# Three-pass products in the output projections and the last graph layer, a mask turned earlier, one transfer asked for earlier

## The reference

```python
x = x + L0_gnn(layernorm(x))    # relu(batchnorm(mean of neighbours @ W_l.T + x @ W_r.T)) + x
x = x + L0_ffn(layernorm(x))    # causal attention, 8 heads of 64:  y = o @ Wo, then a soft mixture of 8 experts
x = x + L1_gnn(layernorm(x))    # 2 graph attention layers:  attn = agg @ Wo[l].T + bo[l]; batchnorm(x + attn) ...
x = x + L1_ffn(layernorm(x))    # 8 experts, top 2 of 8
x = x + L2_gnn(...); x = x + L2_ffn(...)
x = x + L3_gnn(layernorm(x))    # xw = x @ W.T;  out = A_norm @ xw;  gelu(batchnorm(out)) + x
x = x + L3_ffn(layernorm(x))    # 8 experts, top 2 of 8, hidden size 1536
```

## Time and profile before

| | us |
|---|---|
| median of 3 runs (1652.82, 1652.84, 3165.91) | 1652.84 |
| the profiled execution | 1647.62 |
| its span | 1645.4 |
| PE busy | 1580.1 |
| DVE busy | 1233.9 |
| ACT busy | 942.8 |
| POOL busy | 293.5 |

### The profile page before, as it was taken

The page is one execution under the profiler, slowest core; times in us unless marked ns, Lnnn a source line. Parts: engine busy times, 40 slices in busy tenths (PEclk is TensorE's granted clock), DMA queues, the critical chain, the costliest instruction groups (busy, mean ns, idle before and its releaser), DMA issues.

```text
span 1645.4 us, 26288 instructions
## 1 busy us (share of the span) xinstructions
PE 1580.1 (96%) x8703; PEld 1246.9 (76%) x8703; DVE 1233.9 (75%) x2122; ACT 942.8 (57%) x1584; POOL 293.5 (18%) x276
## 2 busy tenths in 40 slices
PE   9997998999999999989999999999999999999998
PEld 8885765878876887568788765865778888888886
DVE  8836662455756475799999868453899999999997
ACT  1423373433644363359999563421578878778784
POOL 0023731010210021198000302000550000000003
PEclk9998998999999999999999999999999999999999
DMA  8010000022001000254952330005264348935003
GB/s 339 20 35 17 1 2 13 1 117 77 1 2 39 1 2 13 116 185 159 343 186 89 102 141 0 1 1 230 63 234 160 130 160 357 390 134 209 19 19 100
DMA packets 42240, 173.15 MB, mean 105 GB/s; under 512 B 10219, under 2 KB 10472, under 8 KB 26681
## 3 DMA queue, kind: packets, MB, share of 16 engines
q1 hardware_dynamic: 28742, 153.75, 24.5%
q0 software_dynamic: 8960, 10.29, 2.3%
q10 hardware_dynamic: 4464, 8.13, 1.3%
HBM read 275.54 MB, written 19.25 MB: 179 GB/s over the span
## 4 chain that ended last, share of the span: by engine, by line
PE 80%; DVE 12%; issue 3%; ACT 2%; DMA 1%; POOL 1%; DVEq 0%; SPq 0%; ACTq 0%; POOLq 0%
PE bank L1097 10%; PE bank L1093 10%; PE bank L1094 10%; PE bank L947 4%; PE bank L919 4%; PE bank L994 4%; PE bank L907 3%; PE bank L859 3%; PE bank L1043 3%; PE bank L1331 3%; PE bank L1223 3%; PE bank L878 2%; PE bank L1396 2%; PE bank L1119 2%; PE bank L1305 2%
## 5 line engine op out<-in xcount | busy, mean ns | idle before, releaser
L719 POOL DMA_INDIRECT sb_W<-slots_out,sb_slus x20 | 30.1, 1503 | 544.8 <-DMA slots_out<-sb_rC 539.3
L1557 ACT ACTIVATE sb_rF<-sb_rF,sb_nmx 125x625 f32<-125x625 f32 (+4 forms) x120 | 89.5, 746 | 45.0 <-DVE sb_nmx L2112 44.9
L657 POOL TENSOR_TENSOR sb_rstd<-sb_ve,sb_half 125x3 f32<-125x3 f32 (+4 forms) x29 | 24.9, 859 | 447.9 <-DVE sb_ve L2016 241.6
L385 DVE TENSOR_TENSOR sb_rA_r<-sb_W,sb_rA_r 128x1024 fp32r<-128x1024 f32 x68 | 83.3, 1226 | 12.1 <-ACT sb_rA_r L1670 12.0
L794 PE MATMUL bank<-sb_ones 128*128 128x512 f32 x184 | 88.5, 628 | 3.8 <-DVE sb_rC L2702 1.3
L2112 DVE CUSTOM_DVE_ANT_0 sb_rF<-bank,sb_rG 125x625 f32<-125x625 f32 x80 | 61.5, 806 | 36.0 <-PE bank L907 35.2
L385 DVE TENSOR_TENSOR sb_rB_r<-sb_W,sb_rB_r 128x1024 fp32r<-128x1024 f32 x68 | 83.4, 1227 | 0.1
L385 DVE TENSOR_TENSOR sb_XT_r<-sb_W,sb_XT_r 128x1024 fp32r<-128x1024 f32 x68 | 83.0, 1220 | 0.2 <-ACT sb_XT_r L1670 0.2
L1670 ACT ACTIVATE sb_rA_r<-sb_W 128x1024 fp32r<-128x1024 f32 x68 | 71.5, 1052 | 14.5 <-DMA sb_W<-in_w_m 11.8
L1705 ACT ACTIVATE sb_rG_r<-bank 128x512 fp32r<-128x512 f32 x51 | 30.5, 598 | 82.0 <-PE bank L1119 82.0
L947 PE MATMUL bank<-sb_rA,sb_rDE 125*64 125x125 f32 x1040 | 69.2, 276 | 4.6 <-DVE sb_rA L2126 4.3
(11 more groups left out here) (549 smaller groups left out, 4795.0 us busy)
## 6 DMA issues: line engine op xcount, KB each, us to landing
sb_W<-in_w_m SPq DMA_DIRECT2D x204, 1024.0 KB
sb_rDE<-in_w_m SPq DMA_DIRECT2D x17, 1024.0 KB
sb_rC<-slots_in SPq DMA_DIRECT2D x33, 256.0 KB, 2.7
sb_W<-in_w_g SPq DMA_DIRECT2D x8, 1024.0 KB, 4.9
slots_out<-sb_rC ACTq DMA_DIRECT2D x31, 256.0 KB, 2.0
slots_in<-sb_rC SPq DMA_DIRECT2D x1, 4608.0 KB, 24.8
sb_W<-in_w_a SPq DMA_DIRECT2D x4, 1024.0 KB, 17.5
sb_W<-in_w_m SPq DMA_DIRECT2D x2, 2048.0 KB, 16.9
```

The costliest lines, as they stand in the source:

```text
L385: eng.tensor_tensor(lo, src[:, HALF * h:HALF * (h + 1)], hi.bitcast(F32), ALU.subtract).then_inc(split(r, p, h, b, "lo")[0], 1)
L1557: act.activation(SM[:, s % 4, 0:kn], SM[:, s % 4, 0:kn], ACT.Exp, scale=-1.0, bias=nmx[:, s:s + 1], accum_out=dens[:, s:s + 1]).then_inc(S ...
```

## The change

- `project_output` replaces `project([(Wo, OT)], ...)` in three places. It multiplies in three passes. OT is split in place at the end of `attention` (`output_high` on ACT, `output_low` on DVE): two pieces of 2 chunks for the tokens that are done, ahead of the last pair's steps, and one for the last tile after the last normalising. Wo is split chunk by chunk in the pair loop, on ACT at p = 5, 7, 9, 11 and on DVE at p = 6, 8, 10, 12. PE starts with a group that does not need the last tile (in the causal case group 1), and asks for the last piece ahead of its second group.
- The last graph layer: ACT and DVE split XT, W3 and AT (W3's high part after the mixture), PE makes both products in three passes; the first product's output is split as it is evicted.
- The mask: 13 of the 25 tiles are turned between groups 2 and 3 of the feature products, with ACT's logarithms after its third eviction, and groups 4 to 7 wait for the bank that each needs; 12 are turned after the last eviction, in place of three `keep` products. The second turning, its wait for `rows_vec` and five further `keep` products go, and eight come after the wait for the logarithms.
- `weights(("y", 0), 1, ...)` is asked for ahead of the scatter wait and `nodes(2)`.

```diff
@@ blocks
                 weights(("a", 1), 1, e, new)
+                weights(("y", 0), 1, e, new)
                 sp.wait_ge(S("sc"), 16 * 2 * T * (r // 2 + 1))
                 nodes(2)
-                weights(("y", 0), 1, e, new)
@@ tensor
+            def project_output(causal, a, full):
+
+                first = 1 if causal else 0
+                pe.wait_ge(S("ot_lo"), a * OT_STEPS + C + 2)
+                for i, j in enumerate((first, 1 - first) + tuple(range(2, len(GROUPS)))):
+                    m, lo, hi = GROUPS[j]
+                    if i == 1:
+                        pe.wait_ge(S("ot_lo"), a * OT_STEPS + C + 3)
+                    n = hi - lo + (hi - lo) % 2
+                    for c in range(C):
+                        for w, x in ((Wo_hi[causal], OT_hi[causal]), (Wo_hi[causal], OT_lo), (Wo_lo, OT_hi[causal])):
+                            mm = pe.matmul(bank[:, j, 0:n], w[c][:, m * P:(m + 1) * P], x[:, c, lo:lo + n],
...
+            def mask_tiles(a, b):
+
+                for at, first, end in MASK_PARTS[a:b]:
+                    for f in range(first, end):
+                        t, k = divmod(f, T)
+                        mm = pe.transpose(bank[0:R, at, (f - first) * P:(f - first) * P + R], AT[:, k, t * R:(t + 1) * R], ident[0:R, 0:R])
+                    mm.then_inc(S("msk_pe"), 1)
+
             for j, (m, lo, hi) in enumerate(GROUPS):
+                if j == 3:
+                    mask_tiles(0, 4)
+                if j >= 4:
+                    pe.wait_ge(S("msk_act"), j - 3)
...
             pe.wait_ge(S("h_done"), 8)
-            keep(7, 3)
+            mask_tiles(4, 7)
+            keep(4, 1)
             to_rows(HB, S("rows_full"), S("bn_out"), 0)
-            keep(7, 2)
-
-            pe.wait_ge(S("rows_vec"), 2 * T)
-            for t in range(T):
-                for k in range(T):
-                    mm = pe.transpose(bank[0:R, t, k * P:k * P + R] if k < 4 else bank[0:R, 5 + t // 4, t % 4 * P:t % 4 * P + R],
-                                      AT[:, k, t * R:(t + 1) * R], ident[0:R, 0:R])
-                mm.then_inc(S("msk_pe"), 1)
-
-
-            keep(7, 3)
-            pe.wait_ge(S("msk_act"), 2 * T)
+            pe.wait_ge(S("msk_act"), len(MASK_PARTS))
+            keep(7, 8)
+
             ln_to_feats(1)
...
+            pe.wait_ge(S("mw_hi"), L3W + 1)
+            for c in range(C):
+                pe.wait_ge(S("mx_hi"), L3X + c + 1)
+                for t in range(T):
+                    pe.matmul(bank[0:R, t, :], x3[0][:, c, t * R:(t + 1) * R], w3[0][:, c], start=(c == 0), stop=False)
+                pe.wait_ge(S("mx_lo"), L3L + c + 1)
+                for t in range(T):
+                    pe.matmul(bank[0:R, t, :], x3[1][:, c, t * R:(t + 1) * R], w3[0][:, c], start=False, stop=False)
+            pe.wait_ge(S("mw_lo"), L3W + 1)
             for t in range(T):
-                row_group(t, XT, t, W3, S("xw_full"))
-            pe.wait_ge(S("xw_done"), 2 + T)
+                for c in range(C):
+                    mm = pe.matmul(bank[0:R, t, :], x3[0][:, c, t * R:(t + 1) * R], w3[1][:, c], start=False, stop=(c == C - 1))
+                mm.then_inc(S("xw_full"), 1)
+            pe.wait_ge(S("mx_hi"), L3X + C + T)
+            pe.wait_ge(S("mx_lo"), L3L + C + T)
             for j, (m, lo, hi) in enumerate(GROUPS):
+                n = hi - lo + (hi - lo) % 2
                 for k in range(T):
-                    mm = pe.matmul(bank[:, j, 0:hi - lo], XW[:, k, m * P:(m + 1) * P], AT[:, k, lo:hi], start=(k == 0), stop=(k == T - 1))
+                    if j == 0:
+                        pe.wait_ge(S("xw_done"), 2 + k + 1)
+                        pe.wait_ge(S("mx_lo"), L3L + C + T + k + 1)
+                    for a, b in ((0, 0), (1, 0), (0, 1)):
+                        mm = pe.matmul(bank[:, j, 0:n], xw3[a][:, k, m * P:(m + 1) * P], at3[b][:, k, lo:lo + n],
@@ scalar, exps
+                    if p == PAIRS:
+                        act.wait_ge(S("at_s"), base(ATT) + ATT)
+                        output_high(0)
+                        output_high(1)
                     if 1 <= p <= PAIRS:
                         turned(p - 1)
                     if p >= 3 and p % 2 == 1:
                         weights((p - 3) // 2)
                     if 1 <= p < PAIRS:
                         exp(2 * p + 1)
+                    if p in (5, 7, 9, 11):
+                        c = (p - 5) // 2
+                        act.wait_ge(S("ld_p3"), base(16) + 16)
+                        act.activation(Wo_hi[causal][c], Wo[:, c], ACT.Copy).then_inc(S("ot_hi"), 1)
+                output_high(2)
@@ vector, attention
                     if 1 <= p <= PAIRS:
                         turned(p - 1)
+                    if p == PAIRS:
+                        output_low(0)
+                        output_low(1)
                     if p >= 3 and p % 2 == 1:
                         normed((p - 3) // 2)
+                    if p in (6, 8, 10, 12):
+                        c = (p - 6) // 2
+                        dve.wait_ge(S("ot_hi"), done + c + 1)
+                        dve.tensor_tensor(Wo_lo[c], Wo[:, c], Wo_hi[causal][c].bitcast(F32), ALU.subtract).then_inc(S("ot_lo"), 1)
+                cn.sync()
+                output_low(2)
@@ vector, last graph layer
             feats(8, XT)
+            for k in range(C):
+                dve.wait_ge(S("mx_hi"), L3X + k + 1)
+                dve.tensor_tensor(x3[1][:, k], XT[:, k], x3[0][:, k].bitcast(F32), ALU.subtract).then_inc(S("mx_lo"), 1)
+            dve.wait_ge(S("mw_hi"), L3W + 1)
+            dve.tensor_tensor(w3[1], W3, w3[0].bitcast(F32), ALU.subtract).then_inc(S("mw_lo"), 1)
+            for t in range(T):
+                dve.wait_ge(S("mx_hi"), L3X + C + t + 1)
+                dve.tensor_tensor(at3[1][:, t], AT[:, t], at3[0][:, t].bitcast(F32), ALU.subtract).then_inc(S("mx_lo"), 1)
             dve.wait_ge(S("ln_vec"), LN[7] + STATS + T)
             add_norm(2 * T)
+            for t in range(T):
+                dve.wait_ge(S("xw_done"), 2 + t + 1)
+                dve.scalar_tensor_tensor(out=xw3[1][:, t], in0=bank[0:R, t, :], scalar=dinvr[:, t:t + 1], in1=xw3[0][:, t].bitcast(F32),
+                                         op0=ALU.mult, op1=ALU.subtract).then_inc(S("mx_lo"), 1)
```

More of the change, by code:

```diff
@@ L871, in project_split @@
                                            start=(c == a == b == 0), stop=(c == C - 1 and a == 1))
+                    mm.then_inc(full, 1)
+            def project_output(causal, a, full):
[9 more added lines that the diff above has]
+                            mm = pe.matmul(bank[:, j, 0:n], w[c][:, m * P:(m + 1) * P], x[:, c, lo:lo + n],
+                                           start=(c == 0 and w is not Wo_lo and x is OT_hi[causal]), stop=(c == C - 1 and w is Wo_lo))
                     mm.then_inc(full, 1)
@@ L1552, in exps, with output_high @@
             def exps(base, causal, last_values):
+                def output_high(i):
+                    part, m = OT_PIECES[i]
+                    lo, hi = OT_PARTS[causal][part]
+                    act.wait_ge(S("at_norm"), base(NORM * T) + NORM * T - (NORM if part == 0 else 0))
+                    act.activation(OT_hi[causal][:, m, lo:hi], OT[:, m, lo:hi], ACT.Copy).then_inc(S("ot_hi"), 1)
                 def exp(s):
@@ L1829, in _, with logs @@
             act.wait_ge(S("ld_small"), 48)
+            def logs(a, b):
+                for i in range(a, b):
+                    at, first, end = MASK_PARTS[i]
+                    act.wait_ge(S("msk_pe"), i + 1)
+                    act.activation(MASK_TILES[:, first:end], bank[0:R, at, :].rearrange("p (k n) -> p k n", n=P)[:, 0:end - first, 0:R],
+                                   ACT.Ln, bias=below[0:R, 1:2]).then_inc(S("msk_act"), 1)
             for j, (m, lo, hi) in enumerate(GROUPS):
```

59 lines of the change are left out of this document (42 added, 17 removed).

## The result

| | before | changed |
|---|---|---|
| median of the runs | 1652.82 (1650.53 to 1652.84) | 1626.84 (1624.58 to 1628.39) |
| profiled execution: time | 1647.62 | 1626.01 |
| its span | 1645.4 | 1623.8 |
| PE busy | 1580.1 | 1564.9 |
| DVE busy | 1233.9 | 1263.0 |

The ratio is 0.9851, with a 95% interval from 0.9837 to 0.9865: 24.6 us less (22.3 to 26.9), 1.5%, so within 2%; the two medians lie 26.0 apart, inside that interval. The forecast was 1629.3. The changed kernel was timed once more with the last experiments: 1625.23, ratio 0.9845 (0.9828 to 0.9861).

A forecast was written before the change was run, and what follows sets the result against it. TensorE (PE) was taken as the bound, with 80% of the span; 2.8 + 7.0 - 0.6 + 7.4 + 4.9 + 2.0 = 23.5 us saved, so 1652.8 - 23.5 = 1629.3 us, range 1616 to 1643.

The forecast's parts named there:

- A projection of 96 rounded products 13.8: Output projections: three rounded passes take 13.8 us against 17.1 for the exact product at full clock, 3.3 saved.
- Causal projection 2.8, the others 3.5 each: Output projections: us saved in the causal attention's (bounds 1 and 3.5) and in each of the two graph attentions'.
- the clock gives more: Rival, chance 0.17: denser PE work raises the granted clock from 142 to 154 and at projection starts; 33 saved, 1620 us.
- POOL held at the causal tail: End of causal attention: POOL's last factor falls beside a DVE subtraction, 0.5 us taken off the saving; 2 more if fully held.
- Splits in the attentions 0.6: Attention loops: splitting the projection weights on ACT and DVE costs 0.2 us per attention, 0.6 for three.
- the covered end: Attention loops: weight splits cost 0 if hidden beside other work, 5.2 us per attention if not; 0.2 was taken.
- covers gone: Rival, chance 0.22: splits don't hide (8 us), POOL is held (2 to 3), the fourth layer stalls (2); 11.5 saved, 1641.
- Fourth layer 7.4: Last graph layer: two three-pass products take 14.0 and 17.2 us, and a wait shrinks; 7.4 us saved, bounds 4 and 8.
- Mask 4.9: Layer 0: normalised rows are turned at 132.8 instead of 138.65; 4.9 us saved after DVE's delay, bounds 2 and 6.
- The 0.9 taken back by DVE's copies: Layer 0 mask: DVE's three copies out queue behind its norms until 134.6, which takes back some 0.9 us.
- Block 1's y0 2.0: Block loop: weights asked for 4.4 us earlier remove ACT's 2.94 wait; 2.0 us saved, bounds -1 and 3.
- The median is 5.2 above the profiled execution: Step from the profiled execution's 1647.62 us to the runs' median, used to forecast from 1652.8 instead of 1624.1 for its like.

## Why the prediction was right, point by point

The total of 23.5 met 24.6, and that is partly luck: by the stages one term was too large (the fourth layer), two too small (projections, mask), and the step from the profiled execution to the median was wrong.

- *A projection of 96 rounded products 13.8.* Right: 14.17 against 13.8 plus the last record's tail (the last one starts 13.9 behind the first), 14.0 for the fourth layer's first product, 17.5 for its second against 17.2 and the same tail. The count of passes alone would have given 12.8: no run shows that. The reason given with it, some 0.012 us beyond the columns, is not in its own rows: 0.115, 0.172 and 0.2325 us for 250, 376 and 512 columns are 0.46, 0.46 and 0.45 ns a column. The sum used the prices and not the reason.
- *Causal projection 2.8, the others 3.5 each.* Measured by stage 3.7, 4.5 and 3.0 with their surroundings. The work itself went as forecast; the surplus is the clock. The second projection begins at the lower level in three of the four traces without the edit, among them, and in none of the ten with it; in half of them the stretch at 286 to 290 and in four the one behind the third projection are gone too. That is the rival *the clock gives more*, come true in part: about 1 to 2 us.
- *POOL held at the causal tail.* Right in size. POOL's last factor and DVE's two subtractions of two SBUF inputs, in the changed kernel:

```profile
247.05 2.73 DVE L2222 TENSOR_TENSOR sb_rB_r<-sb_rB,sb_rDE_r 128x1000 fp32r<-128x1000 f32 x2
```

```profile
247.53 1.19 POOL L699 TENSOR_TENSOR sb_XN<-sb_rden,sb_ones 125x256 f32<-125x256 f32 x1
```

  1.19 us where it took 0.61: 0.6 late, as the 0.5 said (in two other traces it took 1.53). Taken singly, DVE's subtractions run from 247.05 for 1.20 and from 248.17 for 1.61 us; the first ends at 248.25 and POOL 0.47 behind that, at 248.72. In all nine traces in which the subtraction begins first the distance is 0.47, whether POOL's operation took 1.19 or 1.53, and the second subtraction takes 1.61 us. In the run with the splits made twice POOL begins first, 0.16 us ahead: there it takes its 0.61, and the first subtraction 1.51 us instead of 1.20. That is what one sees if whichever begins first is let through and the other waits. The earlier trace rows fits too: POOL L736 ends 2.2 us behind the end of the subtraction beside it (150.54), and takes 2.32 alone. The Trainium skill (GPSIMD Engine Reference, Key points) says that POOL shares its SBUF interfaces with VectorE, with contention where a DVE instruction has two SBUF inputs. The trace agrees, and it does not show the 2 us for both subtractions that the rival counted: by these times POOL waited one out.
- *Splits in the attentions 0.6.* Measured 0.2, all in one of the three. The choice of the covered end was right, and the run with two splits shows that the rival *covers gone* began 0.2 us further on.
- *Fourth layer 7.4.* Inside the layer it is exact: from the end of the product before it to the end of its second product 47.3 us without the edit (mean of four) and 40.0 with it (eight), 7.2 less (40.03 from 47.25). The stage as a whole gives 4.5. What lies ahead of the layer took 185.3 without and 186.8 with it, and what lies behind 32.0 and 33.3. Ahead nothing of the code differs and single traces spread from 184.0 to 188.7: the six with no low stretch there, with or without the edit, took 184.0 to 186.1, the two with 6.8 us of it 188.3 and 188.7. So I count that as chance. Behind, the router's small products meet the low clock earlier. PE's timeline there in the kernel before,

```profile
1155.23 0.65 PE L828 MATMUL bank<-sb_ident,sb_X 125*128 125x125 f32 x4 [0.45 <-DVE sb_X L2097]
1155.71 0.94 PE L834 MATMUL bank<-sb_gw,sb_XT 128*125 128x8 f32 x8
1156.55 0.65 PE L828 MATMUL bank<-sb_ident,sb_X 125*128 125x125 f32 x4
1157.03 2.86 PE L834 MATMUL bank<-sb_gw,sb_XT 128*125 128x8 f32 x16
1159.73 1.20 PE L794 MATMUL bank<-sb_ones 128*128 128x512 f32 x1
```

  and in the changed kernel:

```profile
1133.28 1.10 PE L844 MATMUL bank<-sb_ident,sb_X 125*128 125x125 f32 x4 [0.45 <-DVE sb_X L2177]
1134.17 1.70 PE L850 MATMUL bank<-sb_gw,sb_XT 128*125 128x8 f32 x8
1135.71 1.07 PE L844 MATMUL bank<-sb_ident,sb_X 125*128 125x125 f32 x4
1136.58 3.38 PE L850 MATMUL bank<-sb_gw,sb_XT 128*125 128x8 f32 x16
1139.81 1.20 PE L810 MATMUL bank<-sb_ones 128*128 128x512 f32 x1
```

  The same work takes 4.5 us in the one and 6.5 in the other. What lies behind the layer is 1.2 or more longer in seven of eight traces with the edit and in one of four without it. It goes with the length of the low stretch there: 31.7 to 31.9 us with 6.8 us of it, 33.0 to 33.3 with 10.2, 34.5 with 13.7, and an exception on either side (one with the edit has 6.8, one without it 10.2). What the forecast lacked is this term of 1.3: it asked what the clock does inside the products and not what it does to the work behind them. Timed alone the part gave 8.4 (5.4 to 11.4), which the 7.2 fits and the stage's 4.5 does not, so how much of the 2.7 is chance stays open, and whether the longer low stretch behind is the edit's own too.
- *Mask 4.9.* 6.4 by stage, 5.0 (3.0 to 6.9) timed alone. The turning came at 132.94 for 132.8. The surplus lies ahead of it: the forecast went from one trace of the kernel before, 138.65, and the other three without the edit turn at 139.4 to 140.1. By the means of four and seven the turning comes 7.1 earlier, the heads 6.6, the end of the stage 6.4. The 0.9 taken back by DVE's copies was too large, 0.5 at the heads; and the clock ahead of the turning was no term at all. All four traces without the edit have a low stretch between 128 and 137 (3.4 us in the one that turns at 138.65, 6.8 or 6.9 in the others) and none of those seven has. The stretch before and in the changed kernel (columns as above):

```profile
128.00:137.00 9.00, 7.22 (x31) 5.42 (x31) 5.00 (x12) 2.63 (x7) 1.60 (x2) 0.81 0.00 0
```

```profile
128.00:137.00 9.00, 6.92 (x31) 3.77 (x29) 8.23 (x21) 1.68 (x3) 1.78 (x2) 1.00 0.00 1
```

- *Block 1's y0 2.0.* Right in the traces: 1.95 us from block 0 to block 2 and 1.8 for the loop. Timed alone it was nothing (-0.3, -2.6 to +1.8), which stays open. The prediction looked for the price at the scatter, and there was none: from block 0 to block 2 all eight traces are shorter than any of the four without the edit. It did not ask where the loop waits for transfers anyway. The kernel before shows it, in the stretch of its blocks 7 and 8:

```profile
795.00:823.00 28.00, 27.59 (x131) 21.81 (x130) 26.21 (x32) 25.38 (x42) 0.00 (x0) 1.00 0.97 367
```

  Those blocks vary by 2.4 us between traces, more than the term.
- *The median is 5.2 above the profiled execution.* Wrong as a constant. The changed kernel's median is 0.8 above its profiled execution. The profiled execution before was one of the fastest of its kernel (1647.62; 45 others, 1646.1 to 1655.9), so between the two profiled executions only 21.6 us went. The forecast had 1624.1 for that execution and 1626.01 came. A sum made on a fast execution and carried to a slower median was bound to look too small by some of that difference, and the clock's surplus made it good.

No version beat the changed kernel: the best, with fitted keep-warm products, has 0.9831 (0.9818 to 0.9843) against 0.9845 (0.9828 to 0.9861) on the same chip.

## What to carry to other kernels

Price an edit by the rows of its own stretch, and then compare stages over several executions: here one trace against another of the same kernel differed by up to 3 us in a stage, more than most terms of the sum, and the granted clock of the stretch mostly says why. An engine's idle time of a few tenths covers a split exactly once; count what is left before adding a second. Where a loop streams weights, halve the bytes of the transfers and see what goes: here 2.7 us of three blocks, in a stretch with a DMA share of 0.98, while a stretch at 1.01 kept PE busy throughout. And before one trace is read as "this took back what that gave", look whether the traces without the edit lose the same.

## What the hardware showed that I had not expected

- Two executions of one kernel differ in where the granted clock is low: at 286 to 290 and 672 to 680 it was 0.57 and 0.58 in one and 1.00 in both in the other.
- A mean granted clock of 0.988 instead of 0.985 brought no time that the runs can tell: the two stretches in which it rose were worth some 1 us and under 1 us; eight keep-warm products less, with PE idle for 8.00 us, cost 1.2 us at their place and nothing that the whole shows.
- An operation of POOL that met a subtraction of DVE with two SBUF inputs took 1.19 or 1.53 us instead of 0.61 when it began second, and ended 0.47 us behind the subtraction in all nine traces; the subtraction after it took 1.61 us instead of 1.20. In the one trace in which POOL began first it took 0.61 and the subtraction 1.51.
- With 1 MB transfers one behind the other the DMA share was 0.98 with 369 GB/s in the first block loop, and its transfers cost three blocks 2.7 us; in the second loop it was 1.01 with 421 GB/s.
